# Attention and experts on one core: where the product with V stands in TensorE's order

## The reference, cut to what matters

```
xn  = layernorm(x)
Q, K, V = xn @ W_qkv per head; half of each head's Q and K dimensions is rotated (rope)
S   = where(causal, -inf, Q K^T) / sqrt(64)            # per sequence and head, 256 x 256
O   = softmax(S) V ;  attn = concat_heads(O) @ W_o
ffn = sum over the chosen experts e of gate_e * (gelu(xn w1_e) w2_e) + gate_skip * xn
out = x + attn + ffn
```

## Time and profile before

| | us |
|---|---|
| median of 3 runs (lowest, highest) | 1601.31 (1599.42, 1608.61) |
| the profiled execution | 1614.56, of which span 1612.7 |
| busy in the span: PE, DVE, ACT, POOL | 1267.3 (79%), 1155.0 (72%), 1123.7 (70%), 971.7 (60%) |
| chain that ended last | POOL 30%, PE 20%, issue 18%, DMA 17%, DVE 11%, ACT 2% |
| granted TensorE clock, mean | 0.942 |

### The profile page before, as it was taken

How to read it: one execution, slowest core, us unless ns; L and a number is a source line. 1 busy time by engine, 2 the same in 40 slices (tenths; PEclk the granted TensorE clock), 3 DMA queues, 4 the chain that set the end, 5 groups by cost and what they waited for, 6 DMA issues and landing times.

```text
span 1612.7 us, 46469 instructions
## 1 busy us (share of the span) xinstructions
PE 1267.3 (79%) x13108; PEld 874.4 (54%) x13109; DVE 1155.0 (72%) x4320; ACT 1123.7 (70%) x3606; POOL 971.7 (60%) x1579
## 2 busy tenths in 40 slices
PE   2415877788778878878699999888888888888888
PEld 1303544455444545555498899655555555555555
DVE  6787766666666666667377777777778787877776
ACT  6415666666666767667588888777778777767777
POOL 3245676767677767677200000488778787878776
PEclk9657999999998999999799999999999999999999
DMA  9612222222231322222333323234333333433341
GB/s 288 182 42 63 66 67 65 66 59 72 61 69 44 67 64 65 66 65 67 102 84 85 88 85 85 65 85 96 72 72 74 72 74 74 95 76 75 78 95 33
DMA packets 115784, 129.10 MB, mean 80 GB/s; under 512 B 11568, under 2 KB 75312, under 8 KB 115376
## 3 DMA queue, kind: packets, MB, share of 16 engines
q1 hardware_dynamic: 107056, 110.26, 28.5%
q0 software_dynamic: 8576, 17.33, 3.7%
HBM read 28.85 MB, written 31.59 MB: 37 GB/s over the span
## 4 chain that ended last, share of the span: by engine, by line
POOL 30%; PE 20%; issue 18%; DMA 17%; DVE 11%; ACT 2%; DVEq 1%; POOLq 1%; ACTq 0%; SPq 0%
DMA sorted_x_dram<-stage,rows_at 11%; POOL probs L478 7%; POOL probs L479 7%; PE bank L1081 5%; PE bank L1082 5%; DMA stage<-sorted_y_dram,rows_at 5%; PE bank L1083 4%; POOL arena L462 4%; POOL stage L489 4%; POOL sorted_x_dram L483 3%; POOL arena L461 3%; PE bank L1162 1%; PE bank L1152 1%; PE bank L1216 1%; DVE arena L951 1%
## 5 line engine op out<-in xcount | busy, mean ns | idle before, releaser
L624 ACT ACTIVATE probs<-arena,neg_max 128x128 f32<-128x128 f32 (+1 forms) x1024 | 453.6, 446 | 186.9 <-DVE neg_max L951 178.5
L1162 PE MATMUL bank<-ident,probs 128*128 128x128 f32 x1536 | 276.1, 290 | 165.5 <-POOL probs L479 140.2
L478 POOL TENSOR_TENSOR probs<-probs,inv_total 128x128 f32<-128x128 f32 x512 | 217.1, 424 | 229.6 <-DVE inv_total L958 127.2
L1162 PEld LDWEIGHTS bank<-ident,probs 128*128 128x128 f32 x1536 | 174.9, 145 | 272.6 <-issue 136.1
L951 DVE CUSTOM_DVE_ANT_0 arena<-bank,causal 128x128 f32<-128x128 f32 (+1 forms) x1024 | 315.8, 345 | 2.7 <-PE bank L1152 2.7
L489 POOL DMA_INDIRECT stage<-sorted_y_dram,rows_at x128 | 134.5, 1050 | 263.1 <-DMA sorted_y_dram<-stage 241.4
L479 POOL TENSOR_SCALAR probs<-probs,inv_total 128x256 f32<-128x256 f32 x512 | 274.6, 536 | 0.0
L1152 PE MATMUL bank<-arena 64*128 64x128 f16 (+1 forms) x3072 | 177.1, 250 | 50.6 <-DVE neg_max L951 47.2
L969 DVE TENSOR_TENSOR arena<-bank,arena 128x256 f16<-128x256 f32 x256 | 106.5, 416 | 133.2 <-ACT arena L616 122.3
L624 ACT ACTIVATION_READ_ACCUMULATOR probs<-arena,neg_max 128x1 f32 x1024 | 194.5, 190 | 0.0
L611 ACT ACTIVATE probsT<-bank 128x384 f32<-128x384 f32 x384 | 184.3, 480 | 10.4 <-PE bank L1162 10.2
(11 more groups left out here) (149 smaller groups left out, 2971.4 us busy)
## 6 DMA issues: line engine op xcount, KB each, us to landing
arena<-arena SPq DMA_DIRECT2D x256, 256.0 KB, 5.1
arena<-sorted_x_dram SPq DMA_DIRECT2D x72, 128.0 KB, 2.2
sorted_y_dram<-stage SPq DMA_DIRECT2D x72, 128.0 KB, 1.8
sorted_x_dram<-arena SPq DMA_DIRECT2D x3, 2304.0 KB, 17.9
arena<-experts_dram SPq DMA_DIRECT2D x8, 512.0 KB, 5.1
out_dram<-acc SPq DMA_DIRECT2D x32, 128.0 KB
sorted_x_dram<-arena SPq DMA_DIRECT2D x1, 2368.0 KB, 19.1
sorted_x_dram<-stage,rows_at POOLq DMA_INDIRECT x128, 2.4
```

The lines of the kernel that those rows point to most:

```text
L478: nc.gpsimd.tensor_tensor(p0, p0, inv_total[:, s % 4, 0:1].broadcast_to([P, P]), ALU.mult)
L624: last = nc.scalar.activation(probs[:, s % 4, at:at + w], masked[:, s % 2, at:at + w], ACT.Exp, bias=neg_max[:, s % 2, t:t + 1], scale=-1. ...
L1162: last = nc.tensor.transpose(TP[s % 2][:, k * P:(k + 1) * P], probs[:, s % 4, k * P:(k + 1) * P], ident[:])
```

## The change

In PE's program for a sample, the block that issues `attend` moves up: from behind the transposes to directly behind the scores. `attend` and the scores both fall in even steps only, so in each even step the order scores, projection, transposes, attend becomes scores, attend, projection, transposes. Odd steps, the last steps behind each half (`rest_of`) and all other engines stay as they are. The condition `(s - PV_LAG) % 2 == 1` with `PV_LAG = 5` is met for s = 0, 2, ..., 14; for s up to 4 the product is that of the sample before.

```
                     if s % 2 == 0:
                         scores(b, s, parity, at == OPENING)
+                    if (s - PV_LAG) % 2 == 1:
+                        if s > PV_LAG:
+                            attend(b, (s - PV_LAG) // 2, at)
+                        elif at not in FILLS:
+                            attend(b - 1, (s - PV_LAG + H) // 2, at)
                     for kind, j, u, psum, n in beside(b, at, s):
                         unit(kind, j, owner(kind, b), parity if kind == "v_high" else 1 - parity, psum, before(b, at, n))
                     if not (at in FILLS and s < T_LAG):
                         transposes(G - T_LAG, (s - T_LAG) % 4, None if at == OPENING and s < T_LAG + 2 else
                                    evicted(b, s - T_LAG - 2) if s >= T_LAG + 2 else evicted(b - 1, s - T_LAG - 2 + H))
-                    if (s - PV_LAG) % 2 == 1:
-                        if s > PV_LAG:
-                            attend(b, (s - PV_LAG) // 2, at)
-                        elif at not in FILLS:
-                            attend(b - 1, (s - PV_LAG + H) // 2, at)
```

## The result

The changed kernel takes 1620.94 us in the median of 7 runs (1616.61 to 1626.9), the kernel before 1601.31 us (7 runs beside them, 1599.42 to 1613.34). The ratio, which goes by all the runs and not by the two medians (these alone give 1.0123), is 1.0103 with the interval 1.0066 to 1.0139: slower by 1.0%, some 16 us. On the scale of the prediction that is 1601.3 x 1.0103 = 1617.8 us, near rival 1 (1616 us). The forecast of 1605.6 us did not come; the range for 8 in 10, 1591 to 1618 us, holds the value by 0.2 us. The profiled execution took 1625.13 us (span 1623.3), mean granted clock 0.929 against 0.942.

A forecast was written before the change was run, and what follows sets the result against it. No engine is full, so dependences set the end (POOL 30% of the chain, PE 20%). Terms 1.2 + 3.8 + 1.4 - 2.1 = +4.3 us, 0.27%, took 1601.3 to 1605.6 us; range for 8 in 10: 1591 to 1618 us.

The forecast's parts named there:

- rival 1: The clock decides, at former step 12's second idle: 1.7 us lost in each of 7 samples, 1616 us; chance 0.27.
- The sum over PE's order: Even steps: old and new order both sum to 2.50 us; product starts 1.09 us earlier, projection and transposes 0.81 us later.
- the new neighbours: Product directly behind scores on PE: costed at 0, between -0.1 and +0.14 us for one weight load.
- the 1.1 us: Weight load left open behind the scores, 0.14 us where PE sets the pace: 8 x 0.14, not in the sum.
- rival 2: Waits for the product are real: ACT and DVE freed earlier, a quarter of 67.9 us back, 1584 us; chance 0.11.
- rival 3: Scatters fall differently: half of ten slow ones flip, -10 us, 1591 us; chance 0.06.
- the clock term: Former step 12's second idle grows from 1.34 to 2.15 us, the clock may fall: 7 x 1.0 x 0.55 = 3.8 us.
- 7 samples: Former samples whose successor isn't held at the loop's turn; only in these was a clock fall to cost time.
- The cover that didn't hold: Later projection: ACT reads it one step on, behind its exponentials, so cost 0; uncovered, up to 0.81 us per even step.
- The stall of step 0: Latter half, even samples: product waits 0.63 us for ACT's eviction; bounds 0 and 2.6 us, taken as +1.2 us.
- L1178 waiting for L611: New wait row expected: PE's product waiting for ACT's eviction, about 0.6 us each in the latter half.
- The other small terms of the latter half (+1.4, -2.1): Two more samples might see the clock fall, +1.4 us; a shortened idle spares falls in three odd samples, -2.1 us.

The follow-up runs named there:

- e3: Changed kernel plus 14 unread identity transposes in step 13 of the former samples, filling PE's idle; 1605.45 us, ratio to the kernel before 0.9995.
- e1: Changed kernel, but step 12 keeps the old order (product behind the transposes); 1604.53 us, ratio to the kernel before 0.9995.
- e2: Kernel before, with the product of step 12 alone moved ahead; 1616.76 us, ratio to the kernel before 1.0066.
- e7: Changed kernel, but the product of step 0 stays behind that step's transposes; 1621.6 us, ratio to the kernel before 1.0082.
- e6: Control: changed kernel plus 8 identity transposes in step 9 of the former samples, not step 13; 1625.47 us, ratio to the kernel before 1.011.
- e10: Changed kernel, but the product of step 14 stays behind that step's transposes; 1619.62 us, ratio to the kernel before 1.0051.
- e9: Kernel before, with the product moved ahead in the latter half's samples alone; 1608.7 us, ratio to the kernel before 0.9992.

## Why the prediction was right or wrong, step by step

*What held.* The sum over PE's order: the product starts 0.60 us after the scores, and nothing is lost to the new neighbours, since the projection started 0.60 us after them too. The load of the product's weights in after, sample 5, whose scores start at 364.95:

```profile
365.54 0.20 PEld L1178 LDWEIGHTS bank<-probsT,arena 128*64 128x64 f32 x4 [0.21 <-issue]
```

It begins with the product itself, 0.21 us after the last load for the scores. By the Trainium skill's rule (TensorE: Matmul & The Clock Gate, Part 3, The mechanism) a load stood open there; the trace agrees that it isn't pulled ahead of the scores. But the projection's load did the same behind the scores of before (361.04 in sample 5, again 0.21 us after the last one), so the exchange adds nothing, and the 1.1 us that the prediction set beside its sum weren't there. The wait for L1179 fell and brought nothing; the scatter's wait stayed (95.0 us); in step 10 the 0.4 us gained (5.57 to 5.14 us in the mean) did not shorten the sample; DVE waits longer for the scores. Most of what the earlier trace rows has as waits for the product was thus not on the path, and rival 2 fell, as did rival 3. The lengths of the idles came near the forecast: 1.33 and 2.33 us, where 1.00 and 2.15 were worked out. DVE's wait before L969 was to fall by half or more and fell only from 122.3 to 101.5 us. The sign that the prediction named for its being wrong did come: former samples changed by over 1 us (1.16, after against e3).

*The step that failed: the size of the clock term,* +3.8 us for the former half where some 16 were measured. It had three factors, 7 samples, 1.0 us and a chance of 0.55. Measured are 14, 1.35 us and 12 of 14 (14 x 1.35 x 0.86 = 16.2): all three were too small, the number of samples most of all.

First, the chance. In the samples 1 to 14 of the twelve traces, PE's projection of step 13 ran at full clock in 148. In 78 of these the idle that came next, before the transposes ahead of S(14), was 1.9 us or less, and S(14) was slow in 2 (both in e1, behind 1.69 and 1.86 us). In 70 it was 2.1 us or more, and S(14) was slow in 53. A longer idle went with the fall three times in four. It is no rule for a single one: the same 2.33 us came out both ways in e2, and in before the clock fell in 5 of the 10 samples whose first idle of step 12 was 1.7 us or more. Those 5 stood in the trace that I predicted from; I went by one fall and one that didn't come. The 12 of 14 is itself on the high side: e7, with the order of after in steps 12 to 14, has 8 of 14.

Second, the 7 samples. I left out those whose successor is held at the loop's turn, taking the turn as a fixed point in time. It is not: DVE's hold (2.63 to 3.01 us at the 12 turns of before in which the profile names nothing that it waited for; I had taken some 2) begins when its last instruction of the turn ends. That is `o_low` (L969), behind ACT's `o_high`, which stands behind what ACT evicts late at the lower clock. DVE at the turn from sample 6 to 7 of before (S(0) at 409.63):

```profile
409.40 0.42 DVE L969 TENSOR_TENSOR arena<-bank,arena 128x256 f16<-128x256 f32 x1 [1.24 <-ACT arena L616]
412.75 0.17 DVE L958 RECIPROCAL inv_total<-total 128x2 f32<-128x2 f32 x1 [2.93 <-issue]
```

and at the turn from sample 4 to 5 of after (S(0) at 332.63):

```profile
332.99 0.42 DVE L969 TENSOR_TENSOR arena<-bank,arena 128x256 f16<-128x256 f32 x1 [2.21 <-ACT arena L616]
336.37 0.17 DVE L958 RECIPROCAL inv_total<-total 128x2 f32<-128x2 f32 x1 [2.96 <-issue]
```

The hold is as long, 2.93 and 2.96 us. But L969 ends 0.19 us after S(0) there and 0.78 us after it here, and the next `invert` starts 3.12 us and 3.74 us after it. That is one pair; the six turns between samples 2 and 13 say the same. From S(14) to the first `invert` behind the turn, e3 takes 6.58 to 6.93 us. After takes 7.51 to 8.13 us at the five turns behind a slow S(14), and 6.58 us at the sixth, behind the S(14) of sample 6, which ran at full clock. The late work goes through the turn, so all 14 samples count.

Third, the price of a fall. With 12 falls and the 1.0 us that I had worked out, the term would have been 12 us; measured are some 16, since a fall costs about 1.35 us. The transposes in front of S(14) are slow too (0.90 us instead of 0.55), and I had taken a mixed clock of 0.66 over 5 us, whereas e2 and e6 show 0.50.

*The cover that didn't hold.* I costed the later projection at 0, since ACT reads it after its exponentials. At the lower clock that isn't so: ACT waited 17.1 us for the projection of V (L584 <- L1083) in 20 places, 15 of them in former step 14. In e1 this was 7.6 us, in e2, where the product of step 14 stays behind, there was no such wait in spite of 9 slow S(14), and in e10 it was 0.9:

```profile
ACT arena L584 <- PE bank L1083: 0.9, 1, 0.9
```

Whether that is a cost of its own on the path, e10 doesn't settle: its step 14 is as long as that of after (4.46 us).

*The stall of step 0* (+1.2 us) was next to nothing. In sample 24 of after, the stretch that answers to the earlier trace rows:

```profile
1329.24 0.67 PE L1152 MATMUL bank<-arena 64*128 64x128 f16 x12
...
1329.45 0.50 ACT L611 ACTIVATE probsT<-bank 128x384 f32<-128x384 f32 x1
...
1329.84 0.80 PE L1178 MATMUL bank<-probsT,arena 128*64 128x256 f32 x4
```

The product starts at 1329.84, before the eviction ends at 1329.95. That eviction is of the second head of the pair; `attend` waits for each head by itself, and the first head's matmuls cover most of it: the first half of the product takes 0.80 us instead of 0.66. From S(0) to S(2) the seven even latter samples from 18 on took 3.72 us before, 3.62 after and 3.67 in e7: no loss. The forecast row "L1178 waiting for L611" has 0.6 us in all, on PE's weight loads, not 0.6 each time. The other small terms of the latter half (+1.4, -2.1) can't be told from the scatter of the traces; e9 says that all of the latter half is within 0.4% of nothing.

So the direction of the sum and its largest term were right, the likeliest case was not: what came is the mechanism of rival 1, and its price was right only by luck, from too much per fall (1.7 us) and too few samples (7). That the range for 8 in 10 held is luck too: its upper end went by this price.

## What to carry to other kernels

An operation that is ready and stands between two waits is a spacer: moved out in front, it starts earlier and frees its readers, but the idle behind its old place grows by about its length (1.34 to 2.33 us here, for a product of 0.81), and what follows may run at 1.2 GHz just where PE sets the pace. So add up the new idle of each wait that a moved operation leaves behind, count in the trace what the clock did behind all idles of that length, and ask of each fall whether it lies beside another engine's wait or where PE sets the pace. If it is the latter, keep the order or fill the idle; here that brought the kernel back to where it had been, and no further. A hold that begins when an engine's last instruction ends shields nothing that delays this instruction.

## What was not expected of the hardware

- PE's clock fell behind idles of about 2 us, and not each time: 2 slow S(14) in 78 samples with an idle of up to 1.9 us before it, 53 in 70 with one of 2.1 us or more. The same idle of 2.33 us was followed by a granted clock of 0.50 in sample 3 of e2 and of 1.00 in sample 5.
- Transposes of the identity that nobody reads, 1.69 us of them in each former sample, made after faster by 1% (1.0103 to 0.9995), with the granted clock at 1.00 in the stretch in which it had been 0.66 without them.
- A fall of PE's clock to 0.61 beside another engine's wait cost nothing (7.54 against 7.53 us to the next S(0), e1), one at S(14) some 1.35 us.
- DVE stood 2.6 to 3.0 us at the loop's turn with nothing in the profile that it waited for, whenever its last instruction had ended.
